# Graph attention computed per context token, its rows picked from raw x, and the selection moved behind it

## The reference

```python
# 1: two graph attention layers per batch; the "adjacency" is the layer norm of x
a   = layernorm(x)                                   # 256 x 256 per batch
e   = leaky_relu(self[:, None] + neigh[None, :]) + (-1e10) * (1 - a)
h   = elu(softmax(e) @ (ctx @ W0) + b0)              # 8 heads of 32
g   = elu(softmax(e1) @ (h @ W1) + b1)               # again, same adjacency
x   = x + tanh(g_xattn[0]) * g
# 2: feed-forward, 704 wide
xf  = layernorm(x)
x   = x + tanh(g_ffn[0]) * ((silu(xf @ Gw.T * gs) * (xf @ Uw.T * us)) @ Dw.T * ds)
# 3: selection on ctx: sim = ctx Wq (ctx Wk)^T / 16 per batch, keep the 76 largest of each row
A   = sigmoid(sim) * (sim >= 76th largest of its row)
x   = x + tanh(g_xattn[1]) * ((1 - c) * layernorm(x) + c * (A + A.T) / 2)
# 4: mixture of 8 experts, 2 chosen per token
x   = x + tanh(g_ffn[1]) * moe(layernorm(x))
```

## Time and profile before

| | us |
|---|---|
| median of 3 runs | 294.67 (291.74 to 295.03) |
| the profiled execution, its own time | 290.8 |
| its span, first to last instruction | 289.1 |
| first FFN product (PE, line 1456) starts | 62.60 |
| first down product (PE, line 1467) starts, ends | 87.92, 98.54 |
| second down product starts | 124.57 |

### The profile page before, as it was taken

The page is one execution under the profiler, slowest core; times in us unless marked ns, Lnnn a source line. Parts: engine busy times, 40 slices in busy tenths (PEclk is TensorE's granted clock), DMA queues, the critical chain, the costliest instruction groups (busy, mean ns, idle before and its releaser), DMA issues.

```text
span 289.1 us, 3573 instructions
## 1 busy us (share of the span) xinstructions
PE 231.3 (80%) x1246; PEld 180.7 (63%) x1247; DVE 129.6 (45%) x407; ACT 71.1 (25%) x144; POOL 68.4 (24%) x84
## 2 busy tenths in 40 slices
PE   3979996469988997997071269999999999999950
PEld 3648575344347743575061169998999999986540
DVE  2779558779884478236948832000100100100100
ACT  1444654531120021200032011232123123123210
POOL 5010200100100011000210211355345435545442
PEclk9999999658999999999655559999999999999995
DMA  6797000009920002201950010223322422311200
GB/s 172 268 363 291 0 1 0 3 15 356 415 88 2 0 2 74 73 0 39 362 180 0 19 39 20 36 36 51 63 36 36 60 42 36 53 24 19 25 5 1
DMA packets 15829, 23.88 MB, mean 83 GB/s; under 512 B 4989, under 2 KB 11648, under 8 KB 15808
## 3 DMA queue, kind: packets, MB, share of 16 engines
q1 hardware_dynamic: 10400, 19.02, 18.2%
q0 software_dynamic: 3744, 4.20, 9.1%
q10 hardware_dynamic: 1664, 0.40, 0.6%
HBM read 20.07 MB, written 4.59 MB: 85 GB/s over the span
## 4 chain that ended last, share of the span: by engine, by line
PE 65%; DVE 19%; DMA 4%; issue 3%; POOL 3%; ACT 2%; DVEq 1%; POOLq 0%; ACTq 0%
PE PS L1551 19%; PE PS L1560 9%; PE PS L1467 7%; PE PS L1456 6%; PE PS L1566 4%; DMA zc<-xn_rows,idsu 3%; PE PS L1358 3%; DVE stat L753 2%; PE PS L1436 2%; PE PS L1291 2%; PE PS L1503 2%; PE PS L1544 2%; DVE xn L1055 2%; DVE hT L1074 2%; PE PS L1349 1%
## 5 line engine op out<-in xcount | busy, mean ns | idle before, releaser
L1551 PE MATMUL PS<-hT,e 128*128 128x128 f32 x512 | 64.0, 280 | 0.5 <-ACT hT L681 0.5
L1551 PEld LDWEIGHTS PS<-hT,e 128*128 128x128 f32 x512 | 62.3, 196 | 1.6 <-ACT hT L681 0.9
L1273 DVE TENSOR_TENSOR hT<-th,PS 128x512 f32<-128x512 f32 x19 | 13.1, 687 | 87.9 <-PE PS L1551 73.0
L1456 PE MATMUL PS<-xnT,e 128*128 128x512 f32 x88 | 41.3, 623 | 3.1 <-ACT xnT L644 1.8
L459 POOL TENSOR_TENSOR rstd<-veps,nhalf 128x4 f32<-128x4 f32 (+1 forms) x10 | 9.1, 911 | 119.1 <-DVE veps L758 119.1
L475 POOL DMA_INDIRECT out_dram<-hT,idsu x16 | 25.5, 1591 | 44.0 <-ACT hT L694 41.0
L1456 PEld LDWEIGHTS PS<-xnT,e 128*128 128x128 f32 x88 | 17.1, 200 | 23.5 <-issue 19.6
L1560 PE MATMUL PS<-e,hT 128*128 128x256 f32 x128 | 30.3, 379 | 0.0
L1560 PEld LDWEIGHTS PS<-e,hT 128*128 128x128 f32 x128 | 23.2, 190 | 2.9 <-issue 0.5
L466 POOL DMA_INDIRECT zc<-xn_rows,idsu x16 | 16.9, 1056 | 29.7 <-DVE idsu L1228 18.4
L1467 PE MATMUL PS<-e,hT 128*128 128x256 f32 x96 | 21.3, 381 | 2.1 <-DVE hT L1074 2.1
(11 more groups left out here) (232 smaller groups left out, 285.6 us busy)
## 6 DMA issues: line engine op xcount, KB each, us to landing
e<-e_in SPq DMA_DIRECT2D x24, 512.0 KB, 7.5
x<-x_in SPq DMA_DIRECT2D x2, 512.0 KB, 6.4
e<-gw_in SPq DMA_DIRECT2D x1, 768.0 KB, 9.4
e<-uw_in SPq DMA_DIRECT2D x1, 640.0 KB, 9.2
e<-dw_in SPq DMA_DIRECT2D x1, 640.0 KB, 8.0
out_dram<-x SPq DMA_DIRECT2D x1, 512.0 KB, 2.8
xn_rows<-xn SPq DMA_DIRECT2D x1, 512.0 KB, 3.0
out_dram<-x SPq DMA_DIRECT2D x2, 256.0 KB, 5.3
```

The costliest lines, as they stand in the source:

```text
L1273: dve.tensor_tensor(hh[me], th[:, me, :], PS[:, 2 + me, :], ALU.mult).then_inc(gated, 1)
L1456: mm = pe.matmul(PS[:, bank, :], w[:, k, it * P:(it + 1) * P], xnT[:, h, k, :], start=(k == 0), stop=(k == 1))
L1551: mm = pe.matmul(PS[:, bank + q, f * P:(f + 1) * P], w[:, k * F + f * P:k * F + (f + 1) * P], xgT[q][:, k, :], start=(k == 0), stop=(k == 1))
```

## The change

The graph part is computed in another order of operations. A one-hot product commutes with what is done per token, so both ELU layers are now computed for each context token (`hidden`, `hidden_elu`, `graph_feat`, `graph_elu`), without waiting for the one-hot matrix, and the matrix is applied once at the end, squared (`graph_twice`: hot times hot, in bf16, then `graph_out`). The rows are picked from x itself, which has its maximum where its layer norm has (`pick`: two operations per tile), in bf16. The statistics for the lead check are taken by DVE afterwards (`lead`), and the check's arithmetic is on POOL (`lead_check`). The flag's product and its conversion are a step of their own (`graph_flag`); the branch is read later. `add_graph` adds straight from PSUM, two tiles at a time, and takes the next layer norm's statistics at once. `ctx_s` and its load are gone; ctxT and W0 are loaded first, and the FFN's weights wait for the second half of x.

The list is written anew. The graph part's first half comes first, then the second. `spread`, `count` and `move`, which stood in the graph part, are now among the FFN's steps, `count` is split in two, and `FILL` puts search steps behind `move 2`, `attn_stats 0` and `ffn_up(1, 1)` only. `ffn_up(1, 0)` stands ahead of `move 2` and of `ffn_down(0)`.

```diff
-            FILL = {("move", 2): 3, ("deviation", LN["norm_ffn", 0]): 1, ("graph_check", 1): 6,
-                    ("ffn_up", 0, 0): 4, ("ffn_up", 0, 1): 2, ("ffn_up", 0, 2): 2, ("ffn_up", 0, 3): 4,
-                    ("ffn_up", 0, 4): 5, ("ffn_up", 0, 5): 3, ("ffn_up", 1, 5): 1}
+            FILL = {("move", 2): 5, ("attn_stats", 0): 5, ("ffn_up", 1, 1): 5}
...
+                    ("count", 0, 0), ("turn_ffn", 1), ("ffn_up", 0, 4), ("count", 0, 4), ("move", 1), ("ffn_up", 0, 5),
+                    ("count", 1, 0), ("count", 1, 4), ("ffn_up", 1, 0), ("move", 2), ("ffn_down", 0),
+                    ("attn_stats", 0), ("sigmoids", 0), ("ffn_up", 1, 1), ("ffn_up", 1, 2),
+                    ("lost", 0), ("keep", 0), ("kept", 0), ("attn", 0), ("moe_stats", 0), ("norm_moe", 0),
+                    ("ffn_up", 1, 3), ("keep", 1), ("ffn_up", 1, 4), ("turn_moe", 0),
...
+            def lead_check(h):
+
+                cols = slice(h * HT, (h + 1) * HT)
+                pool.wait_ge(picked_var, h + 1)
+                own(pool.tensor_tensor(grstd[:, cols], gveps[:, cols], nhalf[:, 0:HT], ALU.pow))
+                for n in range(2):
+                    ins = pool.tensor_tensor(lead[:, n, :], top[:, cols, n], gmv[:, cols, 0], ALU.subtract)
+                own(ins)
+                for n in range(2):
+                    ins = pool.tensor_tensor(lead[:, n, :], lead[:, n, :], grstd[:, cols], ALU.mult)
+                own(ins)
...
             def pick(h):
...
                 dve.wait_ge(x_loaded[h], 16)
-                stats(half(x, h))
-                deviations(LN["pick", h])
+                for t in range(h * HT, (h + 1) * HT):
+                    n = mark(dve.max(out=top[:, t, :], in_=x[:, t, :]))
+                after(n)
+                for t in range(h * HT, (h + 1) * HT):
+                    dve.tensor_scalar(hot[:, t, :], x[:, t, :], top[:, t, 0:1], None, ALU.is_ge)\
+                       .then_inc(hot_ready, 1)
...
             def add_graph(h):
...
+                for p in range(2):
+                    t = h * HT + 2 * p
+                    dve.wait_ge(out1_done, 2 * h + p + 1)
+                    xp = x[:, t:t + 2, :].rearrange("p t c -> p (t c)")
+                    dve.scalar_tensor_tensor(out=xp, in0=PS[:, OUT_BANK + p, :], scalar=tg[:, 0:1], in1=xp,
+                                             op0=ALU.mult, op1=ALU.add).then_inc(graph_over, 1)
+                    dve.wait_ge(graph_over, 2 * h + p + 1)
+                    for i in range(2):
+                        ins = dve.bn_stats(stat[:, 2 * p + i, :], x[:, t + i, :])
+                own(ins)
...
+            def hidden(h):
+                if h == 0:
+                    pe.wait_ge(ctx_loaded, 16 * 2)
+                else:
+                    pe.wait_ge(feat_ready, HT)
+                for k in range(2):
+                    pe.matmul(PS[:, 6 + k, :], w0x[:, k * P:(k + 1) * P], ctxT[:, h * HN:(h + 1) * HN],
+                              start=True, stop=True).then_inc(h0_done, 1)
...
+            def graph_twice(h):
+
                 for b in range(2):
+                    pe.wait_ge(hotT_copied, 2 * h + b + 1)
                     for m in range(2):
...
+                        for k in range(2):
+                            mm = pe.matmul(PS[:, HOT_BANK[h] + b, m * 256:(m + 1) * 256],
+                                           hot[:, h * HT + 2 * b + k, m * P:(m + 1) * P],
+                                           hotT[:, 2 * h + b, k, :], start=(k == 0), stop=(k == 1))
+                    mm.then_inc(twiceT_done, 1)
```

More of the change, by code:

```diff
@@ new lines, in build @@
+        SCHEDULE = [("hidden", 0), ("queries", 0), ("hidden_elu", 0), ("pick", 0), ("logits", 0), ("lead", 0),
+                    ("graph_hot", 0), ("graph_feat", 0), ("graph_twice", 0), ("sims", 0), ("graph_elu", 0),
+                    ("gates", 0), ("logit_check", 0), ("graph_flag", 0), ("pick", 1), ("lead", 1), ("graph_out", 0),
+                    ("graph_check", 0), ("add_graph", 0),
+                    ("hidden", 1), ("graph_hot", 1), ("norm_ffn", 0), ("graph_twice", 1), ("hidden_elu", 1),
+                    ("graph_feat", 1), ("turn_ffn", 0), ("graph_elu", 1), ("logit_check", 1), ("scales", 0),
+                    ("ffn_up", 0, 0), ("ffn_up", 0, 1), ("graph_flag", 1), ("graph_out", 1), ("graph_check", 1),
+                    ("add_graph", 1), ("norm_ffn", 1), ("ffn_up", 0, 2), ("spread", 0), ("ffn_up", 0, 3),
+                    ("count", 0, 0), ("turn_ffn", 1), ("ffn_up", 0, 4), ("count", 0, 4), ("move", 1), ("ffn_up", 0, 5),
[3 more added lines that the diff above has]
+                    ("ffn_up", 1, 3), ("keep", 1), ("ffn_up", 1, 4), ("turn_moe", 0),
+                    ("router", 0), ("choices", 0), ("ffn_up", 1, 5), ("kept", 1), ("ffn_down", 1), ("attn_stats", 1),
@@ L349, in build @@
         order = lambda names: {stage: n for n, stage in enumerate(s for s in SCHEDULE if s[0] in names)}
-        LN = order(("pick", "norm_ffn", "attn_stats", "moe_stats"))
+        LN = order(("norm_ffn", "attn_stats", "moe_stats"))
         XT = order(("turn_ffn", "turn_moe"))
@@ L1146, in choices @@
                 own(ins)
-            steps = dict(pick=pick, spread=spread, move=move, keep=keep, kept=kept, scales=scales,
+            steps = dict(pick=pick, lead=lead_stats, add_graph=add_graph, spread=spread, move=move, keep=keep, kept=kept, scales=scales,
                          hidden_elu=hidden_elu, graph_feat=graph_feat,
-                         logit_check=logit_check, graph_elu=graph_elu, graph_check=graph_check, norm_ffn=norm_ffn, ffn_up=ffn_up,
-                         ffn_down=ffn_down, attn_stats=attn_stats, attn=attn, moe_stats=moe_stats, norm_moe=norm_moe,
+                         logit_check=logit_check, graph_elu=graph_elu, graph_flag=graph_flag, graph_check=graph_check,
+                         norm_ffn=norm_ffn, ffn_up=ffn_up, ffn_down=ffn_down, attn_stats=attn_stats, attn=attn, moe_stats=moe_stats, norm_moe=norm_moe,
                          choices=choices)
```

364 lines of the change are left out of this document (196 added, 168 removed).

## The result

The changed kernel takes **312.83 us** (median, 311.47 to 315.41) against 293.21 (290.30 to 295.03) for the kernel before: 1.076 times as long, 95% interval 1.063 to 1.089. The forecast was 311 with a range of 304 to 319. Some executions, of the kernel before too, take over 1.5% longer than the fastest of the same kernel; the ratios leave these out, the medians don't.

What follows compares the result with a forecast made beforehand. It took PE and DVE as both full before the first down product, then PE's queue as bound, after an engine-switching graph chain. Stages of -10.6, +4.4 and +24.3 sum to +18.1: 308.9 or 312.8, forecast 311, range 304 to 319.

Steps and rivals of the forecast that it cites:

- Stage A: Start to the first FFN product: at 52.0 instead of 62.60, a gain of 10.6 us.
- Logits 3.6: Term in PE's opening queue: the logits with their two copies take 3.6 us, plus 0.4 for the last copy.
- `graph_feat` 3.9: Term in PE's queue ahead of the flag: the first half's graph_feat takes 3.9 us.
- one fall of the clock: After 5.4 us of PE idle time, low clock adds 2.2 to graph_feat 1's 3.9 us.
- lower bound of 0.19: Cost of one POOL lead-check operation, from a one-column copy; no loss, against 7.5 us if each cost 1.0.
- Stage B: First FFN product to the first down product's end: at 92.3 instead of 98.54, 4.4 us of the gain lost.
- Stage C: First down product's end to the second down product: 50.4 us instead of 26.0, as DVE's search stands behind the wait.
- the 5.1 of router, half block, silu and last gated rows: Last term ahead of the second down product: 5.1 us, within 7.2 together with transposes and copy.
- two bases: The added 18.1 us on the profiled execution, 290.8, gives 308.9; on the median, 294.67, gives 312.8.
- Rival 1: Slower still: POOL's small operations (+7.5) or skipped branches inside the FFN (+2 each) cost more; 316 to 321, chance 0.09.
- Rival 2: The wait matters less: better overlap (-4), DVE work done under the down product (-6); 299 to 303, chance 0.06.
- Rival 3: Between the down products PE's own queue, not the search, sets the time: -5.4, some 288, chance 0.03.

Runs made afterwards that it cites:

- experiment 7: The changed kernel with sixteen unused 128x128 products put ahead of the logits' small products: 315.48 us, ratio 1.079.
- Experiment 8: The changed kernel with its 8 warm-up products ahead of turn_ffn 0 taken out and 18 put ahead of graph_feat 1: 308.84 us, ratio 1.062.
- the last kernel: The kernel of experiment 10 with the second half's last two FFN products and second down product put ahead of the first half's router: 284.65 us, ratio 0.979.
- experiment 10: The changed kernel with its list rewritten around DVE's queue and the earlier warm-up of Experiment 8 added: 291.84 us, ratio 1.002.
- experiment 2: The changed kernel with a second buffer for the second half's gated rows, so they wait for no down product: 307.46 us, ratio 1.056.

## Why the prediction was right, step by step

**Direction, size and cause were right.** Three of the five signs named for a right forecast are there: DVE idle for 11.47 us ahead of one gated row (10 to 12), PE idle for 19.0 us ahead of `lost` (some 19), 164.4 us at the end (164). The two missed ones are one miss: the first FFN product "near 52", and with it the down product's end "near 92" (96.4).

**Stage A: forecast 52.0, measured 56.47.** The term that was mis-sized is PE's queue from its opening products to the flag, which DVE wrote at 31.44 instead of 27.0. The opening products took 6.3 us and not 5.5 and ended 0.8 late, at a granted clock of 1.00 throughout; in the other traces of this front they took 4.9 to 6.3, and why isn't shown. "Logits 3.6" and the copy's 0.4 measured 5.7 (12.79 to 18.51), and "`graph_feat` 3.9" measured 6.35. Both lie in the stretch from about 14 to 24 us at a granted clock of 1.2 GHz. Behind the flag the forecast held: `add_graph` began at 37.42, the same 4.4 late. The second fall of the clock, from 31 to 35, made `graph_out 0` take 5.31 instead of 3.7, but it stayed covered. It ended at 36.57, and the chain of waits runs through DVE's branch instead (DVEq is DVE's sequencer, L1125 the branch):

```profile
36.02 0.40 DVEq L1125
...
37.33 0.02 DVEq L1021
...
37.42 0.76 DVE x L1023
```

In experiment 7 `graph_out 0` took 3.70, and `graph_feat 1` came no sooner behind the flag's product (14.8 us after it there, 14.9 here). I had priced one fall of the clock, that of `graph_feat 1`, rightly in kind (6.77; forecast 6.1). Experiment 8 filled the idle time ahead of it and the clock held, and so it did in the last kernel; in experiment 10 it fell all the same, so the idle time isn't shown to be the whole cause. What brings the first fall is open: in every trace of this front it came behind the small products, between about 14 and 18 us. That GpSimd would be in time held: `norm_ffn 0`'s power begins 0.1 us after its operand, and a small operation took 0.20 to 0.28 us, near the lower bound of 0.19. Taking that bound had luck in it: the five other copies of one column took 0.74 each in the kernel before, and no row showed a plain operation on four. The Trainium skill ("GPSIMD Engine Reference", Engine selection) has two-input operations at about twice VectorE's time, by my estimate 0.35. At this size that isn't borne out: 0.20 for 128x4 against VectorE's 0.17 for 128x8. The square took 1.04, forecast 1.0.

**Stage B: forecast 29.7 to the down product, measured 29.5.** `hT` was whole at 85.2, 28.7 us after the first FFN product (forecast 28.9), and PE put `ffn_up(1, 0)` into the gap. Branches cost DVE 1.1 to 1.4 (forecast 1.5).

**Stage C: forecast 50.4, measured 52.6.** DVE's chain from the down product to the normalised rows took 43.3 us (96.4 to 139.7), forecast 43.2. The 2.2 over are in the term "the 5.1 of router, half block, silu and last gated rows": it was taken from rows at full clock, and the stretch from the turn at 139.71 to 149.01 is 9.3, not 7.2. Its half block, four instructions, took 3.66 (143.73); the same four take 1.99 at full clock in the first half. This isn't the low clock behind PE's 19 us of idle time, which the forecast had and which was over by 134. The clock fell once more, to 0.50 from about 144 to 147, behind the router's products of 8 columns and two short waits (0.78 and 1.11), and the forecast had no term for that.

**The rest and the rivals.** The end moved by 0.1. The misses of A and C, +4.5 and +2.2, less 0.4 up to the first down product's end and 0.1 at the end, make the 313.4 of the trace out of the 307.2 foreseen for the span; apart from the 0.8 of the opening products they are mostly the clock. The median came nearer (312.8 for 311), and that is partly luck: the profiled execution was the slowest, and the 311 lay halfway between two bases. The forecast added 18.1 us; the traces differ by 24.3 and the medians by 19.6. Rival 1's mechanism (GpSimd, long branches) didn't occur. Rival 2's -6 is real as a number, 5.4 in experiment 2, but the wait was in the kernel. Rival 3's stretch between the down products, 26 us as before, came back in the last kernel alone (89.47 to 115.53). The new check set no flag.

## What to carry to other kernels

A step that waits is paid for by everything queued behind it on its engine: before moving work, ask for each place not what it costs but which wait it will stand behind. Work that was nearly free beside a full engine (here 18.4 us of search, of which 1.5 showed in the traces) costs its full length once it stands behind that engine's result; removing the wait gives back only what stands ahead of the next wait for the same result. And TensorE's clock is part of the price: warm-up products laid into 5 us of idle time kept `graph_feat 1` at full clock in two of three kernels, 2.8 us in experiment 8, and 1.95 more came from taking them off the path where they had stood.
